# In the steady slots VectorE instead of GpSimd makes the low half of the input, two items ahead

## The chip, the core and the metric

The kernel runs on one core of one Trainium2 chip. The metric is the device time of one execution in microseconds (us). Three runs of the kernel before took 1917.87, 1918.23 and 1918.46 us, median 1918.23 us.

## The reference

The network reads 2048 sequences of 50 steps with 128 features, and one "news" vector for each sequence. Cut to what matters:

```python
hs  = gru(hist, gru_W, gru_U, gru_b)              # 50 steps, 128 units: z, r, candidate
emb = concat([hs, news - hs, news, hs * news])    # attention on each step
a   = relu(emb @ att_W1 + b1); a = relu(a @ att_W2 + b2)
ats = sigmoid(a @ att_W3 + b3)                    # one score for each step and sequence

def au_step(h, xs):                               # second recurrence, over the GRU's states
    u = sigmoid(xu + h @ au_Uu); r = sigmoid(xr + h @ au_Ur)
    c = tanh(xc + r * (h @ au_Uc))
    u_ = at * u
    return (1 - u_) * h + u_ * c
x = batch_norm(concat([h_final, news]))
y = sigmoid(leaky(leaky(x @ d_W1 + d_b1) @ d_W2 + d_b2) @ f_W + f_b)
```

All is float32. The kernel keeps this accuracy by writing a float32 operand as the sum of two float16 halves, `hi` (the value rounded) and `lo` (the value less `hi`), and each weight in the same way. A product is then three float16 products: hi by hi, hi by lo, lo by hi.

## The kernel before

The 2048 sequences are four chunks of 512 (`NC`, `CH`). An item is one chunk at one time step, so there are 200 items, numbered in the order step, chunk: item `i` is chunk `i % 4` at step `i // 4`. The features lie on the 128 partitions and the 512 sequences along the free dimension, so that every elementwise operation works on a 128x512 tile.

The program is written out by hand for each of the five engines, with no scheduler. Each engine runs its own list in order, and semaphores (`wait_ge`, `then_inc`) join the lists. Apart from a short start (items 0 to 13, functions `early`) and an end (`late`, and the dense head), the lists consist of slots, one for each item from 14 (`EARLY`) to 199. Slot `low` does the GRU step of item `low`, the first attention layer of item `low - 2`, and the second recurrence for item `low - 10` (`LAG`) and its neighbours. The loop over slots is unrolled; one slot in four also holds the second attention layer of four items and their scores.

What TensorE does in a slot is fixed in order (lines 1333 to 1400): the attention layer of item `low - 2` (`attention_1`), the reset gate (weights `W_R` on the input x, `U_R` on the state h), the update gate of the second recurrence (`GW_U`, `GU_U`), the candidate's input part, the reset gate and candidate of the second recurrence, the GRU's update gate (`W_Z`, `U_Z`), and two more products. Each product is six matmuls of 64 by 512, two at a time on the two halves of the array. Counted from the code, a slot has 84 of them, and the longer slot 16 more. TensorE waits for `xlo_ready` before the reset gate (line 1343), and for `h_ready` of the item before ahead of `GW_U` (line 1353), since that product overwrites the PSUM bank in which the former update gate stands.

ScalarE does the sigmoids and tanhs and makes most of the `hi` halves. For the input it makes `x_hi` of item `low + 3` in slot `low` (`input_high`, line 682). VectorE does the elementwise steps that read PSUM. GpSimd has no PSUM operand anywhere in this kernel; in a slot it runs, in this order (lines 406 to 425):

- `g_lo`, the low half of the second recurrence's state (line 409),
- `hn`, state times news (line 327), which waits for VectorE's new state h,
- `gus`, update gate times score (line 416),
- `hn_lo` (line 333) and `h_lo` (line 339), low halves, which wait for ScalarE's high halves,
- `d`, old state less candidate (line 423), which VectorE needs for the new state,
- `x_lo`, the low half of the input of item `low + 1` (line 346).

On VectorE the part of a slot around the change is, in order: `a_lo` (line 867), `gt`, reset gate times a product of the second recurrence (line 1027, waits for `gr_ready` from ScalarE), `d` times the update gate z (line 1033, waits for `d_ready` from GpSimd and `z_ready` from ScalarE), a second `gt` step (line 1038) and the new state h (line 1041, which releases `h_ready`). All of these read at least one operand from PSUM.

SyncE's list loads the input: `load_step` waits until `xlo_ready` says that the chunk's buffer in `x32` has been split, and then loads the item four further on. After the third chunk of each step its list also has the two transfers that spread the scores over the partitions, and those wait for scores and for `gus_ready`.

Of the kernel before, what the change touches and what calls it, by code (L numbers as in the profile page):

```python
# [24 lines left out]
ALU = mybir.AluOpType  # L25
# [8 lines left out]
NC = 4  # L34
# [43 lines left out]
def rec_kernel(nc, xs, pack_gru, pack_state, pack_att, pack_rest, out):  # L78
# [14 lines left out]
    EARLY = LAG + NC  # L93
# [6 lines left out]
    def has(item):  # L100
        return 0 <= item < ITEMS

    def pairs_of(low):
        return low % NC == TILED % NC and has(low - TILED)
# [18 lines left out]
    def att_bank(item):  # L123
        return B_GXH if isinstance(item, int) and item < 2 * NC and item % 2 == 0 else B_A1
# [3 lines left out]
    with ExitStack() as ctx:  # L128
        def sb(name, shape, dt=F32):
            return ctx.enter_context(nc.sbuf_tensor(name, shape, dt))  # L130

        def sem(name):
            return ctx.enter_context(nc.semaphore(name))
# [18 lines left out]
        x32 = sb("x32", [P, NC, CH])  # L152
        x_hi = sb("x_hi", [P, NC, CH], F16)
        x_lo = sb("x_lo", [P, NC, CH], F16)
# [61 lines left out]
        xhi_ready, xlo_ready = sem("xhi_ready"), sem("xlo_ready")  # L216
# [99 lines left out]
        def _(pool):  # L316
# [4 lines left out]
            def state_news(item, count):  # L321

                c, k = item % NC, item % 2
                if isinstance(item, int) and item < NC:
                    pool.wait_ge(news_landed[c], 16)
                pool.wait_ge(h_ready, count)
                g.tensor_tensor(hn[:, k, :], h32[:, c, :], news[:, c, :], ALU.mult).then_inc(hn_ready, 1)  # L327

            def state_news_low(item, count):

                k = item % 2
                pool.wait_ge(hnhi_ready, count)
                g.tensor_tensor(hn_lo[:, item % NC, :], hn[:, k, :], hn_hi[:, item % NC, :], ALU.subtract).then_inc(hnlo_ready, 1)  # L333
# [8 lines left out]
            def input_low(item, count):  # L342

                c = item % NC
                pool.wait_ge(xhi_ready, count)
                g.tensor_tensor(x_lo[:, c, :], x32[:, c, :], x_hi[:, c, :], ALU.subtract).then_inc(xlo_ready, 1)  # L346
# [50 lines left out]
            def slot(s0, off):  # L397
                low = off + (s0 if isinstance(s0, int) else LOOP_LO)

                def at(lag):  # L400
                    return s0 + (off - lag + 1)

                def landed(lag):
                    return 4 * (s0 + (off - lag - (low - lag) % NC)) + 16

                if has(low - LAG - 4) and has(low - LAG - 4 + NC):
                    c = (low - LAG - 4) % NC
                    pool.wait_ge(ghi_ready, at(LAG + 4))
                    g.tensor_tensor(g_lo[:, c, :], g32[:, c, :], g_hi[:, c, :], ALU.subtract).then_inc(glo_ready, 1)
                if has(low - 1):  # L410
                    state_news(low - 1, at(1))
                if has(low - LAG - 1):
                    c, k = (low - LAG - 1) % NC, (low - LAG - 1) % 2
                    pool.wait_ge(gu_ready, at(LAG + 1))
                    pool.wait_ge(score_landed, landed(LAG + 1))
                    g.tensor_tensor(gus[:, k, :], gu[:, k, :], score[:, c, :], ALU.mult).then_inc(gus_ready, 1)  # L416
                if has(low - 1):
                    state_news_low(low - 1, at(1))
                    state_low(low - 1, at(1))
                if has(low):  # L420
                    c, k = low % NC, low % 2
                    pool.wait_ge(hc_ready, at(0))
                    g.tensor_tensor(d[:, k, :], h32[:, c, :], hc[:, k, :], ALU.subtract).then_inc(d_ready, EARLY + 1 if low == EARLY else 1)  # L423
                if has(low + 1) and low > EARLY:
                    input_low(low + 1, at(-1))

            for s in range(1, EARLY):
                if s == NC:
# [385 lines left out]
        def _(dve):  # L814
            v = nc.vector
# [47 lines left out]
            def attention_1_low(item, count):  # L863

                k = item % NC
                dve.wait_ge(a1hi_ready, count)
                v.scalar_tensor_tensor(out=a1_lo[:, k, :], in0=ps[:, att_bank(item), :], scalar=0.0,
                                       in1=a1_hi[:, k, :], op0=ALU.max, op1=ALU.subtract).then_inc(a1lo_ready, 1)
# [98 lines left out]
            def slot(s0, off):  # L967
                low = off + (s0 if isinstance(s0, int) else LOOP_LO)

                def at(lag):  # L970
                    return s0 + (off - lag + 1)

                def late(lag):
                    return s0 + (off - lag + 1 - NC)

                if pairs_of(low - 1):
                    low_2(0, paired(s0 + (off - 1)))
                if has(low - 2):
                    attention_1_news(low - 2, at(2))
                if low > EARLY and has(low - LAG - 1):  # L980
                    gated_difference(low - LAG - 1, at(LAG + 1))
                if low > EARLY and pairs_of(low - 1):
                    low_2(1, paired(s0 + (off - 1)))
                if has(low):
                    k = low % 2
                    dve.wait_ge(hh_pe, late(0))
                    dve.wait_ge(r_ready, at(0))
                    v.scalar_tensor_tensor(out=t[:, k, :], in0=ps[:, B_HH, :], scalar=b_hs,
                                           in1=r[:, k, :], op0=ALU.add, op1=ALU.mult).then_inc(t1_ready, 1)
                if low == EARLY:  # L990
                    gated_first(low - LAG - 1, at(LAG + 1))
                elif has(low - LAG - 1):
                    gated_step(low - LAG - 1, at(LAG + 1))
                if has(low):
                    k = low % 2
                    dve.wait_ge(t1_ready, at(0))
                    dve.wait_ge(xh_pe, at(0))
                    v.tensor_tensor(t[:, k, :], t[:, k, :], ps[:, B_XH, :], ALU.add).then_inc(t2_ready, 1)
                if low == EARLY:
                    low_2(1, paired(low - 1))  # L1000
                if low > EARLY and has(low - LAG - 1):
                    gated_state(low - LAG - 1, at(LAG + 1))
                if has(low - 2):
                    attention_1_low(low - 2, at(2))
                known = low if isinstance(s0, int) else None
                if known == BN_LO:
                    bn_eps()
                if known == BN_LO + 1:
                    bn_guess()
                for i in range(NEWTON):  # L1010
                    if known == BN_LO + 3 * i + 2:
                        bn_square(i)
                    if known == BN_LO + 3 * i + 3:
                        bn_error(i)
                    if known == BN_LO + 3 * i + 4:
                        bn_root(i)
                if known == BN_LO + 3 * NEWTON + 2:
                    bn_scale()
                if known == BN_LO + 3 * NEWTON + 3:
                    bn_mean()  # L1020
                if known == BN_LO + 3 * NEWTON + 4:
                    bn_shift()
                if has(low - LAG):
                    k = (low - LAG) % 2
                    dve.wait_ge(ghh_pe, late(LAG))
                    dve.wait_ge(gr_ready, late(LAG))
                    v.tensor_tensor(gt[:, k, :], gr[:, k, :], ps[:, B_GHH, :], ALU.mult).then_inc(gt1_ready, 1)  # L1027
                if known == BN_LO:
                    bn_shift_bits()
                if has(low):  # L1030
                    dve.wait_ge(d_ready, at(0))
                    dve.wait_ge(z_ready, at(0))
                    v.tensor_tensor(ps[:, B_Z, :], d[:, low % 2, :], ps[:, B_Z, :], ALU.mult).then_inc(e_ready, 1)
                if has(low - LAG):
                    k = (low - LAG) % 2
                    dve.wait_ge(gxh_pe, at(LAG))
                    dve.wait_ge(gt1_ready, late(LAG))
                    v.tensor_tensor(gt[:, k, :], gt[:, k, :], ps[:, B_GXH, :], ALU.add).then_inc(gt2_ready, 1)  # L1038
                if has(low):
                    dve.wait_ge(e_ready, at(0))  # L1040
                    v.tensor_tensor(h32[:, low % NC, :], hc[:, low % 2, :], ps[:, B_Z, :], ALU.add).then_inc(h_ready, 1)  # L1041
# [546 lines left out]
```

## Time and profile before

| what | value |
|---|---|
| median of three runs | 1918.23 us (1917.87 to 1918.46) |
| profiled execution, its time | 1917.94 us |
| its span, first to last instruction | 1916.1 us |
| TensorE (PE) busy | 1908.0 us, 100% |
| GpSimd (POOL) busy | 1645.4 us, 86% |
| VectorE (DVE) busy | 1473.6 us, 77% |
| ScalarE (ACT) busy | 1471.6 us, 77% |
| granted TensorE clock | 1.00 through the span |

The time of the profiled execution is 1.84 us more than its span, for what lies ahead of the first and behind the last instruction. An engine's share is its busy time over the span. A row of the timeline gives an instruction's start, its duration, the engine, the line and the tiles; what stands in brackets at its end is the time that the engine sat idle before it, and what it waited for. Durations of successive instructions overlap by a little (the next one begins before the last result of the former is written): VectorE begins one every 0.60 us where it has no wait, though each lasts 0.68 us. The order of the waits is therefore read from starts and ends together.

### The profile page before, as it was taken

The numbers are of one execution on the slowest core, as the hardware profiler recorded it, in microseconds if no ns is written. First come the engines' busy times: TensorE is split into PE (matmuls) and PEld (weight loads), VectorE is DVE, ScalarE is ACT, GpSimd is POOL, SyncE is SP. The second block draws the span as 40 slices with busy tenths as digits, with TensorE's granted clock in tenths as the row PEclk, the third lists the DMA queues.
The fourth block names the chain that finished last, engine by engine and source line by source line (L and its number), as shares of the span: only waits on it lengthen the run. The fifth ranks groups of instructions, "written<-read, shape, count | busy, mean of one in ns | idle before, by whom it ended". The sixth has DMA issues, their size and how long they took to land.

```text
span 1916.1 us, 44510 instructions
## 1 busy us (share of the span) xinstructions
PE 1908.0 (100%) x17607; PEld 999.3 (52%) x17607; DVE 1473.6 (77%) x2324; ACT 1471.6 (77%) x2484; POOL 1645.4 (86%) x1409
## 2 busy tenths in 40 slices
PE   9999999999999999999999999999999999999999
PEld 4555555555555555555555555555555555555554
DVE  7777777777777777777777777777777777787777
ACT  7877777777777777777777777777777777777777
POOL 7888888888888888888888888888888888888886
PEclk9999999999999999999999999999999999999999
DMA  4211121112111211121121112111211121112110
GB/s 131 69 55 53 55 69 54 51 51 73 51 51 51 73 51 50 54 70 50 51 69 55 50 51 73 51 54 53 70 53 51 51 73 51 51 51 73 45 46 23
DMA packets 37911, 110.67 MB, mean 58 GB/s; under 512 B 4348, under 2 KB 4732, under 8 KB 31304
## 3 DMA queue, kind: packets, MB, share of 16 engines
q1 hardware_dynamic: 37560, 107.57, 17.4%
q8 instruction: 140, 2.29, 0.5%
q14 instruction: 67, 0.55, 0.1%
q10 hardware_dynamic: 144, 0.26, 0.1%
HBM read 107.40 MB, written 0.42 MB: 56 GB/s over the span
## 4 chain that ended last, share of the span: by engine, by line
PE 94%; ACT 2%; DVE 1%; POOL 1%; issue 1%; DMA 0%; SPq 0%; DVEq 0%; ACTq 0%; POOLq 0%
PE ps L1149 88%; PE ps L1232 3%; PE ps L1150 1%; PE ps L1223 1%; POOL hn_lo L333 0%; POOL h_lo L339 0%; DMA x<-in_xs 0%; DVE ps L885 0%; DVE ps L879 0%; ACT ps L752 0%; POOL hn L327 0%; ACT ps L575 0%; ACT g_hi L736 0%; ACT a_hi L512 0%; DVE g L890 0%
## 5 line engine op out<-in xcount | busy, mean ns | idle before, releaser
L1149 PE MATMUL ps<-h_hi,w_hi 128*64 128x512 f16 x1384 | 524.6, 379 | 1.9 <-POOL h_lo L339 1.4
L1150 PE MATMUL ps<-h_hi,w_hi 128*64 128x512 f16 x1384 | 524.7, 379 | 0.0
L1150 PE MATMUL ps<-h_lo,w_hi 128*64 128x512 f16 x1384 | 524.5, 379 | 0.0
L1150 PE MATMUL ps<-h_hi,w_lo 128*64 128x512 f16 x1384 | 524.5, 379 | 0.0
L1149 PE MATMUL ps<-h_hi,w_lo 128*64 128x512 f16 x1384 | 524.5, 379 | 0.0
L1149 PE MATMUL ps<-h_lo,w_hi 128*64 128x512 f16 x1384 | 524.5, 379 | 0.0
L333 POOL TENSOR_TENSOR hn_lo<-hn,hn_hi 128x512 f16<-128x512 f32 x200 | 232.4, 1162 | 162.2 <-ACT hn_hi L507 161.8
L327 POOL TENSOR_TENSOR hn<-h,news 128x512 f32<-128x512 f32 x200 | 255.0, 1275 | 74.3 <-DVE h L1041 74.3
L662 ACT ACTIVATE ps<-gt,p_rest 128x512 f32<-128x512 f32 x185 | 127.7, 690 | 199.4 <-DVE gt L1038 199.4
L346 POOL TENSOR_TENSOR x_lo<-x,x_hi 128x512 f16<-128x512 f32 x196 | 226.9, 1158 | 11.8 <-ACT x_hi L527 11.8
L416 POOL TENSOR_TENSOR gus<-gu,score 128x512 f32<-128x512 f32 x186 | 237.0, 1274 | 0.0
L423 POOL TENSOR_TENSOR d<-h,hc 128x512 f32<-128x512 f32 x186 | 236.8, 1273 | 0.0
L1027 DVE TENSOR_TENSOR gt<-gr,ps 128x512 f32<-128x512 f32 x186 | 128.0, 688 | 138.5 <-ACT gr L693 138.5
L339 POOL TENSOR_TENSOR h_lo<-h,h_hi 128x512 f16<-128x512 f32 x200 | 233.2, 1166 | 0.4 <-ACT h_hi L502 0.3
L1149 PE MATMUL ps<-x_hi,w_hi 128*64 128x512 f16 x605 | 229.3, 379 | 0.6 <-DVE a_lo L856 0.6
L1150 PE MATMUL ps<-x_hi,w_hi 128*64 128x512 f16 x605 | 229.3, 379 | 0.0
L1149 PE MATMUL ps<-x_lo,w_hi 128*64 128x512 f16 x605 | 229.3, 379 | 0.0
L1150 PE MATMUL ps<-x_lo,w_hi 128*64 128x512 f16 x605 | 229.3, 379 | 0.0
L1149 PE MATMUL ps<-x_hi,w_lo 128*64 128x512 f16 x605 | 229.3, 379 | 0.0
L1150 PE MATMUL ps<-x_hi,w_lo 128*64 128x512 f16 x605 | 229.3, 379 | 0.0
L1149 PEld LDWEIGHTS ps<-h_hi,w_hi 128*64 128x64 f16 x1384 | 152.2, 110 | 146.1 <-issue 3.0
L1149 PE MATMUL ps<-g_hi,w_hi 128*64 128x512 f16 x596 | 225.9, 379 | 1.1 <-DVE g_lo L1097 1.1
(191 smaller groups left out, 6756.4 us busy)
## 6 DMA issues: line engine op xcount, KB each, us to landing
x<-in_xs SPq DMA_DIRECT2D x199, 256.0 KB, 3.0
score<-score_rows SPq DMA_DIRECT2D x48, 1024.0 KB, 4.7
news<-in_xs SPq DMA_DIRECT2D x4, 256.0 KB, 5.3
x<-score_rows SPq DMA_DIRECT2D x1, 1024.0 KB, 4.6
h<-score_rows SPq DMA_DIRECT2D x1, 1024.0 KB, 5.1
score_rows<-s_rows SPq DMA_DIRECT2D x50, 8.0 KB
p_rest<-in_pack_rest SPq DMA_DIRECT2D x1, 776.0 KB, 7.0
p_att<-in_pack_att SPq DMA_DIRECT2D x1, 291.0 KB, 5.3
```

The costliest lines, as they stand in the source:

```text
L327: g.tensor_tensor(hn[:, k, :], h32[:, c, :], news[:, c, :], ALU.mult).then_inc(hn_ready, 1)
L333: g.tensor_tensor(hn_lo[:, item % NC, :], hn[:, k, :], hn_hi[:, item % NC, :], ALU.subtract).then_inc(hnlo_ready, 1)
L339: g.tensor_tensor(h_lo[:, item % HIST, :], h32[:, c, :], h_hi[:, item % HIST, :], ALU.subtract).then_inc(hlo_ready, 1)
L346: g.tensor_tensor(x_lo[:, c, :], x32[:, c, :], x_hi[:, c, :], ALU.subtract).then_inc(xlo_ready, 1)
L416: g.tensor_tensor(gus[:, k, :], gu[:, k, :], score[:, c, :], ALU.mult).then_inc(gus_ready, 1)
L423: g.tensor_tensor(d[:, k, :], h32[:, c, :], hc[:, k, :], ALU.subtract).then_inc(d_ready, EARLY + 1 if low == EARLY else 1)
L662: a.activation(ps[:, B_GXH, :], gt[:, (low - LAG - 1) % 2, :], ACT.Tanh, bias=b_gated[:, 2:3]).then_inc(gc_ready, 1)
L1027: v.tensor_tensor(gt[:, k, :], gr[:, k, :], ps[:, B_GHH, :], ALU.mult).then_inc(gt1_ready, 1)
L1149: m.matmul(ps[0:H, bank, :], weights[:, 0:H], moving, start=start, stop=stop)
L1150: return m.matmul(ps[H:P, bank, :], weights[:, H:P], moving, start=start, stop=stop)
L1223: done = m.matmul(ps[p * H:(p + 1) * H, bank, :], w3_pair[:, :], part[:, p, :], start=part is a2_hi, stop=part is a2_lo)
L1232: done = m.matmul(ps[k * H:(k + 1) * H, B_PAIR[p], :], w[:, A_2, 0:H], a1[:, 2 * p + k, :], start=w is w_hi and a1 is a1_hi, stop=a1 is a1_lo)
```

## The change

In the slots, `x_lo` moves from GpSimd to VectorE, and one item further ahead: GpSimd made it for item `low + 1` as the last thing of its slot; now VectorE makes it for item `low + 2`, between `a_lo` and `gt`. In slot 14 the new instruction also waits until GpSimd's own last `x_lo` (item 15, in the start) is done. The start (`early`) is unchanged, so items up to 15 are split as before. ScalarE, TensorE and SyncE have the same lists; the lines below the change are numbered four higher.

```diff
@@ GpSimd, slot
                     g.tensor_tensor(d[:, k, :], h32[:, c, :], hc[:, k, :], ALU.subtract).then_inc(d_ready, EARLY + 1 if low == EARLY else 1)
-                if has(low + 1) and low > EARLY:
-                    input_low(low + 1, at(-1))
@@ VectorE, slot
                 if has(low - 2):
                     attention_1_low(low - 2, at(2))
+                if has(low + 2):
+                    c = (low + 2) % NC
+                    dve.wait_ge(xhi_ready, at(-2))
+                    if low == EARLY:
+                        dve.wait_ge(xlo_ready, low + 2)
+                    v.tensor_tensor(x_lo[:, c, :], x32[:, c, :], x_hi[:, c, :], ALU.subtract).then_inc(xlo_ready, 1)
```

VectorE's list in an ordinary slot before, from `a_lo` to the new state:

```order
L867 SCALAR_TENSOR_TENSOR a_lo<-ps,a_hi 128x512 [waits a1hi_ready]
L1027 TENSOR_TENSOR gt<-gr,ps 128x512 [waits gr_ready,ghh_pe]
L1033 TENSOR_TENSOR ps<-d,ps 128x512 [waits z_ready,d_ready]
L1038 TENSOR_TENSOR gt<-gt,ps 128x512 [waits gt1_ready,gxh_pe]
L1041 TENSOR_TENSOR h<-hc,ps 128x512 [waits e_ready]
```

And the same place of VectorE's list now:

```order
L865 SCALAR_TENSOR_TENSOR a_lo<-ps,a_hi 128x512 [waits a1hi_ready]
L1008 TENSOR_TENSOR x_lo<-x,x_hi 128x512 [waits xhi_ready]
L1031 TENSOR_TENSOR gt<-gr,ps 128x512 [waits gr_ready,ghh_pe]
L1037 TENSOR_TENSOR ps<-d,ps 128x512 [waits z_ready,d_ready]
L1042 TENSOR_TENSOR gt<-gt,ps 128x512 [waits gt1_ready,gxh_pe]
L1045 TENSOR_TENSOR h<-hc,ps 128x512 [waits e_ready]
```

One instruction is new, ahead of the four that lead to the state. Both of its inputs lie in SBUF; the other five have one in PSUM.

GpSimd's list before, from the end of one slot into the next:

```order
L339 TENSOR_TENSOR h_lo<-h,h_hi 128x512 [waits hhi_ready]
L423 TENSOR_TENSOR d<-h,hc 128x512 [waits hc_ready]
L346 TENSOR_TENSOR x_lo<-x,x_hi 128x512 [waits xhi_ready]
L409 TENSOR_TENSOR g_lo<-g,g_hi 128x512 [waits ghi_ready]
L327 TENSOR_TENSOR hn<-h,news 128x512 [waits h_ready]
```

And GpSimd's list now:

```order
L339 TENSOR_TENSOR h_lo<-h,h_hi 128x512 [waits hhi_ready]
L423 TENSOR_TENSOR d<-h,hc 128x512 [waits hc_ready]
L409 TENSOR_TENSOR g_lo<-g,g_hi 128x512 [waits ghi_ready]
L327 TENSOR_TENSOR hn<-h,news 128x512 [waits h_ready]
L416 TENSOR_TENSOR gus<-gu,score 128x512 [waits score_landed,gu_ready]
```

`g_lo` follows `d` directly, and a slot of GpSimd has six instructions where it had seven. The whole of VectorE's list has 184 instructions more (2323 before, 2507 now) and GpSimd's 184 fewer.

## Rows read from the trace of the kernel before

**Rows 1.** The page's first part: busy time, share of the span, instructions.

```profile
PE 1908.0 (100%) x17607; PEld 999.3 (52%) x17607; DVE 1473.6 (77%) x2324; ACT 1471.6 (77%) x2484; POOL 1645.4 (86%) x1409
```

**Rows 2.** Busy time by stretch: from:to, length, each engine's busy us, clock, DMA.

```profile
95.00:105.00 10.00, 9.72 (x90) 5.11 (x88) 7.79 (x13) 7.33 (x13) 9.12 (x9) 1.00 0.21 83
...
122.92:160.90 37.98, 37.98 (x354) 19.95 (x352) 29.18 (x47) 29.04 (x49) 33.02 (x29) 1.00 0.17 57
```

**Rows 3.** Timeline, TensorE in a steady slot: start, duration, tiles (one half each).

```profile
1132.42 0.38 PE L1149 MATMUL ps<-h_hi,w_hi 128*64 128x512 f16 x1
...
1132.63 0.38 PE L1149 MATMUL ps<-h_lo,w_hi 128*64 128x512 f16 x1
...
1132.85 0.38 PE L1149 MATMUL ps<-h_hi,w_lo 128*64 128x512 f16 x1
...
1133.07 0.38 PE L1149 MATMUL ps<-h_hi,w_hi 128*64 128x512 f16 x1
```

**Rows 4.** Timeline, VectorE in the same ordinary slot, from a_lo to the state.

```profile
1127.46 0.69 DVE L867 SCALAR_TENSOR_TENSOR a_lo<-ps,a_hi 128x512 f16<-128x512 f32 x1
1128.90 0.69 DVE L1027 TENSOR_TENSOR gt<-gr,ps 128x512 f32<-128x512 f32 x1 [0.75 <-ACT gr L693]
1130.15 0.69 DVE L1033 TENSOR_TENSOR ps<-d,ps 128x512 f32<-128x512 f32 x1 [0.56 <-ACT ps L696]
1130.76 0.68 DVE L1038 TENSOR_TENSOR gt<-gt,ps 128x512 f32<-128x512 f32 x1
1131.36 0.68 DVE L1041 TENSOR_TENSOR h<-hc,ps 128x512 f32<-128x512 f32 x1
```

**Rows 5.** Timeline, GpSimd beside it.

```profile
1127.11 1.16 POOL L339 TENSOR_TENSOR h_lo<-h,h_hi 128x512 f16<-128x512 f32 x1
1128.22 1.27 POOL L423 TENSOR_TENSOR d<-h,hc 128x512 f32<-128x512 f32 x1
1129.45 1.16 POOL L346 TENSOR_TENSOR x_lo<-x,x_hi 128x512 f16<-128x512 f32 x1
1130.57 1.16 POOL L409 TENSOR_TENSOR g_lo<-g,g_hi 128x512 f16<-128x512 f32 x1
1132.12 1.28 POOL L327 TENSOR_TENSOR hn<-h,news 128x512 f32<-128x512 f32 x1 [0.39 <-DVE h L1041]
```

**Rows 6.** Timeline, ScalarE beside it: the gates for which VectorE waits.

```profile
1128.13 0.67 ACT L693 ACTIVATE gr<-ps,p_rest 128x512 f32<-128x512 f32 x1
...
1129.39 0.66 ACT L696 ACTIVATE ps<-ps,b_zr 128x512 f32<-128x512 f32 x1 [0.59 <-PE ps L1150]
```

**Rows 7.** Timeline of the start: VectorE's own x_lo (L1056), with GpSimd beside it.

```profile
17.95 0.68 DVE L1056 TENSOR_TENSOR x_lo<-x,x_hi 128x512 f16<-128x512 f32 x1
...
19.61 1.27 POOL L327 TENSOR_TENSOR hn<-h,news 128x512 f32<-128x512 f32 x1
20.05 1.38 DVE L1056 TENSOR_TENSOR x_lo<-x,x_hi 128x512 f16<-128x512 f32 x1 [1.42 <-ACT x_hi L527]
20.84 1.60 POOL L339 TENSOR_TENSOR h_lo<-h,h_hi 128x512 f16<-128x512 f32 x1
```

**Rows 8.** Timeline of slot 14, the first one, and TensorE behind it.

```profile
93.97 1.16 POOL L339 TENSOR_TENSOR h_lo<-h,h_hi 128x512 f16<-128x512 f32 x1
93.98 0.68 DVE L867 SCALAR_TENSOR_TENSOR a_lo<-ps,a_hi 128x512 f16<-128x512 f32 x1
95.09 1.27 POOL L423 TENSOR_TENSOR d<-h,hc 128x512 f32<-128x512 f32 x1
...
96.40 0.70 DVE L1033 TENSOR_TENSOR ps<-d,ps 128x512 f32<-128x512 f32 x1
...
97.60 0.68 DVE L1041 TENSOR_TENSOR h<-hc,ps 128x512 f32<-128x512 f32 x1
...
98.34 0.40 PE L1149 MATMUL ps<-h_hi,w_hi 128*64 128x512 f16 x1 [0.28 <-DVE h L1041]
```

**Rows 9.** Timeline, GpSimd in the longer slot of the same period.

```profile
1116.92 1.16 POOL L333 TENSOR_TENSOR hn_lo<-hn,hn_hi 128x512 f16<-128x512 f32 x1 [2.16 <-ACT hn_hi L507]
```

## The prediction

> **What bounds the kernel now.** I read the shares first, then the busy time by stretch, then the timeline of one period, engine by engine. The shares put TensorE at 100% and GpSimd, from which work is taken, at 86% [rows 1]. By stretch, a steady period of four slots lasts 37.98 us, and TensorE is busy in all of it, GpSimd in 33.02, VectorE in 29.18 [rows 2]. The timeline confirms that this is a bound and no waiting in disguise: matmuls start every 0.215 us, two at a time, whether the next one reads h_hi, h_lo or begins another product [rows 3]. An engine that waited for an operand would show a longer step somewhere.
>
> The Trainium skill (Perfetto Trace Analysis, Identifying the Most-Contended Engine) speaks against reading it so: matmuls are pipelined, so their busy time misleads, and the busy share of the weight loads is the better measure. That share is 52% here [rows 1]; the even step of 0.215 us is what decides against the rule, since it leaves no gap for another engine to close.
>
> What can be lost or won is therefore a question of slack. In the steady slot the nearest consumer on TensorE is the product that waits for `h_ready`. VectorE ends h at 1131.36 + 0.68 = 1132.04, and TensorE starts that product at 1133.07, from its own order and without a wait [rows 3, 4]. So h may come up to 1.03 us later before TensorE loses anything.
>
> **The change part by part.**
>
> *GpSimd loses x_lo.* 184 instructions of 1.16 us go, a step of 1.12 us each from 1129.45 to 1130.57 [rows 5]. Behind it stand `g_lo` and then `hn`, and `hn` already waits 0.39 us for h [rows 5]. So the freed time turns into a longer wait ahead of `hn`, and no consumer gets anything sooner by it except x_lo itself. It is worth nothing, as TensorE waits for none of GpSimd's results in the period. SyncE's loads wait on `xlo_ready` and go out about a slot earlier; nothing in a full TensorE period can use that either.
>
> *VectorE gains x_lo.* The trace has the same operation on VectorE in the start. Undisturbed it takes 0.68 us. Once it met a GpSimd instruction: it started at 20.05, GpSimd's `hn` ended at 19.61 + 1.27 = 20.88, and x_lo ended at 21.43, 0.55 us behind that. GpSimd's next instruction, queued with no gap, took 1.60 us in place of 1.16, or 0.44 more [rows 5, 7]. So the two engines exclude each other for this form. VectorE waits for the GpSimd instruction that runs, goes next, and the following GpSimd instruction is held for 0.44 us.
>
> The Trainium skill (SBUF — State Buffer, Who interferes with whom) says this as a rule: a VectorE instruction with two SBUF inputs and a GpSimd instruction that reads SBUF exclude each other on a shared port, and whichever issues second is blocked until the first ends. The rows agree for that single meeting. The page does not say who goes next when GpSimd has more queued; both answers are worked out below.
>
> Now the steady slot. `a_lo` starts at 1127.46, and VectorE's step is 0.60 us (1130.76 to 1131.36), so x_lo would ask at 1128.06 [rows 4]. GpSimd then runs `h_lo`, until 1127.11 + 1.16 = 1128.27 [rows 5]. x_lo ends at 1128.27 + 0.55 = 1128.82. The next on VectorE, `gt`, waits for ScalarE's gate until 1128.13 + 0.67 = 1128.80, and started at 1128.90 after 0.75 us of idling [rows 4, 6]. With the overlap of 0.08 between instructions it could start at 1128.74 behind x_lo; so it stays at 1128.90. The 0.75 us wait is the cover, and it is nearly used up.
>
> The `d` on GpSimd is held 0.44 us and ends at 1128.22 + 1.27 + 0.44 = 1129.93 [rows 5]. VectorE needs it at line 1033, but also z, which ScalarE ends at 1129.39 + 0.66 = 1130.05 [rows 6]. z is still later, by 0.12 us. Hence h ends at 1132.04 as before, and the slot costs 0. The longer slot has the same order behind `a_lo`; there GpSimd's `hn_lo` sits 2.16 us until ScalarE's `hn_hi` [rows 9], so that a late GpSimd is put right once in four slots.
>
> *The first slot.* Here there is no cover: the chain runs through GpSimd's `d` to h and TensorE, which stood 0.28 us for h [rows 8]. x_lo asks at 93.98 + 0.60 = 94.58, `h_lo` ends at 95.13, and `d` is held 0.44 us, until 95.09 + 1.27 + 0.44 = 96.80. Lines 1033 and 1041 and TensorE's product at 98.34 each move by 0.44. `gt` between them needs x_lo's end at 95.68, which is sooner than that. This is the only term: +0.44 us.
>
> *Sum.* Against the profiled execution's 1917.94 us: 184 slots at 0, and 0.44 once, gives 1918.38, say 1918.4 us. The median of the runs shown, 1918.23, lies 0.29 above the profiled time, so in terms of the runs the forecast is 1918.4 to 1918.7; the runs themselves spread over 0.59 us.
>
> *Bounds.* The unknown cost is one x_lo on VectorE beside a GpSimd that has more queued. The nearest rows are 0.68 and 1.38 us [rows 7]; I take 0.76, from 1128.06 to 1128.82, because it meets only the last 0.21 us of `h_lo`. It asks just 0.16 us ahead of `d` (1128.06 against 1128.22), and if it loses that race it waits for all of `d`. The end on that side: x_lo ends at 1128.22 + 1.27 + 0.55 = 1130.04, `gt` starts at 1129.96, lines 1033, 1038 and 1041 follow in steps of 0.60, and h starts at 1131.76, 0.40 late. That leaves 0.63 of the 1.03 us: still 0 for TensorE in a steady slot. In the first slots, where there is less slack, up to three slots may pay it: 3 x 0.40 = 1.20 more, or 1919.6. On the other side the most that TensorE could get back between 95 and 105 us is its idle 0.28 us [rows 2], or 1917.7.
>
> **The rivals.**
>
> *x_lo loses the race to `d` in most slots.* For it speaks the margin of 0.16 us. Then VectorE's x_lo shows about 1.9 us long and h is 0.40 late, and the time is 1918.4 to 1919.6, since the 1.03 us holds. The kernel would stand closer to its edge with nothing to show for it in time.
>
> *GpSimd keeps the port while it has work queued: slower.* Then x_lo waits through `d` and the `g_lo` that now follows it directly, until GpSimd stops for h. `g_lo` would run from 1129.45 to 1130.61, x_lo end at 1131.16, and h at 1131.16 - 0.08 + 3 x 0.60 + 0.68 = 1133.56, behind TensorE's 1133.07. From there each slot is a closed ring: h, six GpSimd instructions, x_lo, four on VectorE, h. GpSimd's mean is 33.02 over 28 in the period, 1.18 us, and six are 7.08; then 0.55, then 2.40 from x_lo's end to h's, and 0.08 from h to `hn`: 10.11 us. TensorE's mean slot is 37.98 / 4 = 9.50. The loss is 0.61 x 184 = 112 us, or 2030 us. It decides as soon as VectorE is not served between two queued GpSimd instructions. Against it: at 20.84 `h_lo` was queued behind `hn` with no gap, and VectorE went between [rows 7]. But that is one meeting, and here there are 184.
>
> *TensorE has room, and the freed GpSimd gives time: faster.* At most it could give GpSimd's whole step, 1.12 x 184 = 206 us, or 1712 us; a tenth of it would be seen. The even step of the matmuls [rows 3] and `hn`'s wait for h [rows 5] speak against any of it.
>
> **How the numbers follow.** The forecast case has 0.65. Losing the race to `d` has 0.23. The held port has 0.08, and with it lies all of slower. Faster has 0.02. The last 0.02 is for a gain of the 0.28 us, which no run could tell. A measurement of this kernel tells about 0.2%, or 3.8 us, from no change, so the first two cases and the last are "same": 0.90. The range takes the bounds 1917.7 and 1919.6 with the spread of the runs, 0.59, on either side: 1917.1 to 1920.2. The held port, 112 us away, is left out.
>
> **What the new profile would show.** If right: TensorE's steady period is still 37.98 us and its step 0.215; VectorE has an x_lo of about 0.76 us between `a_lo` and `gt`, and the 0.75 us wait for `gr` is all but gone; `d` on GpSimd lasts about 1.7 us; `hn` waits for h 1.0 to 1.1 us in place of 0.39; and TensorE's idle at 98 us grows from 0.28 to about 0.72. An x_lo of about 1.9 us with `d` at 1.27 and `g_lo` longer would be the lost race. x_lo ending only behind `g_lo`, and TensorE waiting for h in every slot, would make the prediction wrong.

## The result, and the profile after

The changed kernel takes 1925.21 us (median of five executions, 1925.15 to 1926.93). Beside it on the same chip the kernel before takes 1918.23 us (1917.50 to 1920.19). The ratio is 1.0038, with a 95% interval of 1.0026 to 1.0049. So the change makes the kernel slower by some 7 us. The forecast of 1918.4 us was wrong, and the upper end of its range, 1920.2, was missed by 5.0 us.

The profiled execution of the changed kernel took 1925.15 us, its span is 1923.4 us. Against the profiled execution of before that is 7.21 us more. The page's first part answers to [rows 1]:

```profile
PE 1909.3 (99%) x17607; PEld 999.1 (52%) x17607; DVE 1619.6 (84%) x2508; ACT 1468.2 (76%) x2484; POOL 1523.6 (79%) x1225
```

TensorE has the same work and is no longer at 100%. The list of waits (engine, line, waited for: us in total, times, longest) says for whom it now stands (it lists idle time of over 0.15 us):

```profile
POOL hn L327 <- DVE h L1045: 215.7, 186, 2.5
...
PE ps L1153 <- DVE h L1045: 5.5, 7, 0.8
```

Before, TensorE waited once for the new state h, 0.28 us [rows 8]. Now it waits seven times. The busy time by stretch (from:to, length, busy us of PE, PEld, DVE, ACT, POOL, clock, DMA share, GB/s) tells where:

```profile
1149.20:1187.18 37.98, 37.98 (x354) 19.95 (x352) 31.82 (x51) 29.05 (x49) 30.35 (x25) 1.00 0.17 56
...
1756.99:1794.98 37.99, 36.34 (x334) 18.52 (x332) 35.99 (x52) 26.81 (x48) 28.08 (x23) 1.00 0.17 57
```

The first row answers to the period of [rows 2]: TensorE is full, as before. Fifteen successive stretches of this length, from 1149.20 to 1719.00, read so. The three after them, to 1832.96, read like the second row: TensorE lacks 1.6 us in each, and 18 to 20 of its matmuls no longer fit in. The loss lies in three of the last periods, and in one slot at the beginning.

This is an ordinary steady slot of the changed kernel, VectorE, GpSimd and the TensorE product that needs h, in the timeline; it answers to [rows 3 to 5]:

```profile
140.46 0.69 DVE L865 SCALAR_TENSOR_TENSOR a_lo<-ps,a_hi 128x512 f16<-128x512 f32 x1
141.06 0.74 DVE L1008 TENSOR_TENSOR x_lo<-x,x_hi 128x512 f16<-128x512 f32 x1
141.21 1.73 POOL L423 TENSOR_TENSOR d<-h,hc 128x512 f32<-128x512 f32 x1
141.90 0.69 DVE L1031 TENSOR_TENSOR gt<-gr,ps 128x512 f32<-128x512 f32 x1
142.90 1.16 POOL L409 TENSOR_TENSOR g_lo<-g,g_hi 128x512 f16<-128x512 f32 x1
143.15 0.69 DVE L1037 TENSOR_TENSOR ps<-d,ps 128x512 f32<-128x512 f32 x1 [0.56 <-ACT ps L694]
...
144.35 0.68 DVE L1045 TENSOR_TENSOR h<-hc,ps 128x512 f32<-128x512 f32 x1
...
145.11 1.28 POOL L327 TENSOR_TENSOR hn<-h,news 128x512 f32<-128x512 f32 x1 [1.06 <-DVE h L1045]
...
146.06 0.38 PE L1153 MATMUL ps<-h_hi,w_hi 128*64 128x512 f16 x1
```

It is the slot that was forecast, to the hundredths: x_lo 0.74 us, d held to 1.73, z still the later one ahead of line 1037, `hn` waiting 1.06, and h ending at 145.03, 1.03 us before TensorE's product. Slot 14 is the forecast one too (answers to [rows 8]):

```profile
94.77 1.11 DVE L1008 TENSOR_TENSOR x_lo<-x,x_hi 128x512 f16<-128x512 f32 x1
95.28 1.73 POOL L423 TENSOR_TENSOR d<-h,hc 128x512 f32<-128x512 f32 x1
...
97.04 0.70 DVE L1037 TENSOR_TENSOR ps<-d,ps 128x512 f32<-128x512 f32 x1 [0.57 <-POOL d L423]
...
98.98 0.40 PE L1153 MATMUL ps<-h_hi,w_hi 128*64 128x512 f16 x1 [0.73 <-DVE h L1045]
```

TensorE's idle time there grew from 0.28 to 0.73, or 0.45 us. That leaves 7.21 - 0.45 = 6.8 us for the late periods. There a slot of the changed kernel looks so:

```profile
1731.79 0.68 DVE L1045 TENSOR_TENSOR h<-hc,ps 128x512 f32<-128x512 f32 x1
1732.54 1.28 POOL L327 TENSOR_TENSOR hn<-h,news 128x512 f32<-128x512 f32 x1 [1.37 <-DVE h L1045]
...
1736.96 0.69 DVE L865 SCALAR_TENSOR_TENSOR a_lo<-ps,a_hi 128x512 f16<-128x512 f32 x1
1737.28 1.27 POOL L423 TENSOR_TENSOR d<-h,hc 128x512 f32<-128x512 f32 x1
1737.56 1.54 DVE L1008 TENSOR_TENSOR x_lo<-x,x_hi 128x512 f16<-128x512 f32 x1
1738.51 1.60 POOL L409 TENSOR_TENSOR g_lo<-g,g_hi 128x512 f16<-128x512 f32 x1
1739.02 1.11 DVE L911 SCALAR_TENSOR_TENSOR bn_t<-bn_t 128x2 f32<-128x2 f32 x1
1740.06 0.67 DVE L1031 TENSOR_TENSOR gt<-gr,ps 128x512 f32<-128x512 f32 x1
...
1741.39 0.38 PE L1153 MATMUL ps<-h_hi,w_lo 128*64 128x512 f16 x1
1741.85 0.68 DVE L1045 TENSOR_TENSOR h<-hc,ps 128x512 f32<-128x512 f32 x1
...
1742.58 0.40 PE L1153 MATMUL ps<-h_hi,w_hi 128*64 128x512 f16 x1 [0.80 <-DVE h L1045]
```

Between x_lo and `gt` stands an instruction that the prediction did not count: a step of the batch norm's inverse root, two values on each partition. The functions `bn_eps` to `bn_shift` (lines 895 to 928) are such steps, and one of them stands in each slot from 184 to 197 (`BN_LO`; slot 184 has a second one behind `gt`), in the code behind the new x_lo and ahead of `gt`. The same step in the timeline of the kernel before:

```profile
1735.85 0.21 DVE L913 SCALAR_TENSOR_TENSOR bn_t<-bn_t 128x2 f32<-128x2 f32 x1
1736.01 1.27 POOL L423 TENSOR_TENSOR d<-h,hc 128x512 f32<-128x512 f32 x1
1736.69 0.69 DVE L1027 TENSOR_TENSOR gt<-gr,ps 128x512 f32<-128x512 f32 x1 [0.62 <-ACT gr L693]
```

It took 0.21 us in the wait for the gate, just ahead of d. Now it takes 1.11. Both of its inputs lie in SBUF, as those of x_lo do, and it has to wait for GpSimd as x_lo does. An instruction is said to ask when it starts in the timeline. x_lo asks behind d and waits for it, and by the time that the small step asks, `g_lo` has asked already: the step waits until `g_lo` ends. From a_lo to h it takes 1741.85 - 1736.96 = 4.89 us where the ordinary slot takes 144.35 - 140.46 = 3.89, so h is 1.00 us later on that path. One such slot alone would still fit into the 1.03 us of slack; the loss comes from handing the delay on. GpSimd waits for h with `hn`, then runs without a gap to the end of `g_lo`, `g_lo` holds the small step, and the small step holds the next h. That closes a ring, a chain in which each h waits for the one before: h starts at 1721.75, 1731.79, 1741.85 and 1751.90, one every 10.05 us, where TensorE's mean slot is 9.50. Four turns are 40.2 us in place of 37.99, and TensorE's waits show the same distance: one period after the row at 1742.58 comes

```profile
1782.78 0.40 PE L1153 MATMUL ps<-h_hi,w_hi 128*64 128x512 f16 x1 [0.80 <-DVE h L1045]
```

or 40.20 us later, and the next comes at 1823.00, 40.22 after that. Three such periods (12 slots) cost 3 x 2.22 = 6.7 us; with slot 14's 0.45 that is 7.1 of the 7.21.

The waits in the list are shorter than the loss, because they count only from the end of the matmul before. From start to start, TensorE's step is 1742.58 - 1741.39 = 1.19 us in place of 0.215, or 0.97 more. That happens in two slots of a late period. In a third the step is 0.43 us (1772.30 to 1772.73), too little idle time for the list. Together 0.97 + 0.97 + 0.21 = 2.15 of the 2.22 us. In the longer slot of each late period the chain is another: x_lo asks ahead of d there, the small step waits for d (1.22 us), and GpSimd waits 1.08 us for ScalarE's `hn_hi`. Why h comes after some 10.05 us in that slot too, no run here shows.

### The profile page after: what moved, and what is told of

Its sections match the earlier page's. It is cut to its first block, busy times and chain, and to the rows that moved or that the text cites. A ratio compares the mean times of both kernels' runs of the same rounds, so it can differ in the third digit from the quotient of the medians.

```text
span 1923.4 us, 44511 instructions
## 1 busy us (share of the span) xinstructions
PE 1909.3 (99%) x17607; PEld 999.1 (52%) x17607; DVE 1619.6 (84%) x2508; ACT 1468.2 (76%) x2484; POOL 1523.6 (79%) x1225
## 4 chain that ended last, share of the span: by engine, by line
PE 89%; POOL 4%; ACT 3%; DVE 2%; issue 2%; DMA 0%; SPq 0%; DVEq 0%; POOLq 0%; ACTq 0%
PE ps L1153 83%; PE ps L1236 3%; PE ps L1154 1%; PE ps L1227 1%; POOL hn L327 1%; POOL hn_lo L333 1%; POOL h_lo L339 1%; POOL d L423 1%; POOL g_lo L409 0%; POOL gus L416 0%; ACT ps L573 0%; DVE gt L1042 0%; DMA x<-in_xs 0%; ACT a_hi L510 0%; POOL x_lo L346 0%
## 5 line engine op out<-in xcount | busy, mean ns | idle before, releaser
L423 POOL TENSOR_TENSOR d<-h,hc 128x512 f32<-128x512 f32 x186 | 312.2, 1678 | 0.0
L1153 PE MATMUL ps<-g_hi,w_hi 128*64 128x512 f16 x596 | 225.9, 379 | 1.1 <-DVE g_lo L1101 1.1
L1154 PE MATMUL ps<-g_hi,w_hi 128*64 128x512 f16 x596 | 225.9, 379 | 0.0
L1153 PE MATMUL ps<-g_lo,w_hi 128*64 128x512 f16 x596 | 225.9, 379 | 0.0
```

Source lines behind the costliest of these rows:

```text
L1153: m.matmul(ps[0:H, bank, :], weights[:, 0:H], moving, start=start, stop=stop)
L1154: return m.matmul(ps[H:P, bank, :], weights[:, H:P], moving, start=start, stop=stop)
```

## Experiments

The theory after the result: the loss is the batch norm's steps behind x_lo, because VectorE then meets GpSimd twice ahead of `gt`, and a slot has room for one such meeting in which VectorE has to wait. I held at first that the number of meetings counts, whatever their order; the first rival is that the order of asking decides. Others are that x_lo alone is too much, that anything more on VectorE behind x_lo would do the same, and that the engines take turns.

**The batch norm's steps elsewhere (e1).** They go from behind x_lo to VectorE's wait for the reset gate r, half a slot earlier.

```diff
                 if low > EARLY and has(low - LAG - 1):
                     gated_difference(low - LAG - 1, at(LAG + 1))
+                known = low if isinstance(s0, int) else None
+                if known == BN_LO:
+                    bn_eps()
...
@@ behind x_lo
-                known = low if isinstance(s0, int) else None
-                if known == BN_LO:
-                    bn_eps()
...
```

> The changed kernel, with the small batch-norm instructions of slots 184 to 197 (128x2, one a slot) moved to a place ahead of VectorE's wait for r, away from x_lo. Theory (port): TensorE's loss between 1719 and 1833 us comes from two VectorE instructions in a row that each have to let one GpSimd instruction by; with x_lo alone each slot pays one, and the loss of 6.7 us goes. Expected 1918.3 to 1919.2 us: the before plus the 0.45 of slot 14; no wait of TensorE for h after 100 us. Rival (load): VectorE is simply too full with x_lo and the small ones in these slots; moving them within the slot changes nothing, 1925 us.

Measured: 1918.74 us (1918.08 to 1920.65), ratio to before 1.0004, interval 0.9995 to 1.0013. The step and what follows it in VectorE's list, and the stretch that had lacked 1.6 us:

```profile
1734.47 0.22 DVE L911 SCALAR_TENSOR_TENSOR bn_t<-bn_t 128x2 f32<-128x2 f32 x1
...
1735.36 0.75 DVE L1004 SCALAR_TENSOR_TENSOR t<-ps,p_gru,r 128x512 f32<-128x512 f32 x1 [0.67 <-ACT r L645]
```

```profile
1719.00:1756.99 37.99, 37.99 (x354) 19.95 (x352) 32.29 (x55) 29.05 (x50) 30.37 (x25) 1.00 0.17 57
```

The step is back at 0.22 us with 0.67 us of idling behind it, TensorE is full, and its only wait for h is the one of slot 14. The 6.7 us are gone with nothing else moved: it was these steps behind x_lo, not x_lo alone.

**The steps ahead of x_lo (e2).** The same block directly between a_lo and x_lo; number and kind of the meetings stay.

```diff
                     attention_1_low(low - 2, at(2))
+                known = low if isinstance(s0, int) else None
+                if known == BN_LO:
+                    bn_eps()
...
                 if has(low + 2):
                     c = (low + 2) % NC
...
-                known = low if isinstance(s0, int) else None
...
```

> The changed kernel, with the small batch-norm instructions between a_lo and x_lo, so that x_lo follows them. Theory (port): the number of meetings counts and not their order; the small one waits for d, then x_lo for g_lo, which costs 0.44 us a slot more than the other order, because the longer of the two now comes last. Expected as slow as the change or slower, 1925 to 1930 us. Rival (order): the small instruction is the one that comes too late behind x_lo; ahead of it, it takes 0.22 us in the end of h_lo and the loss goes, 1918.3 to 1920 us.

Measured: 1918.66 us (1918.20 to 1920.33), ratio 1.0004, interval 0.9995 to 1.0013. My theory, that the number of meetings counts, fell here; the rival, that the order decides, held. The timeline:

```profile
1738.19 0.21 DVE L911 SCALAR_TENSOR_TENSOR bn_t<-bn_t 128x2 f32<-128x2 f32 x1
1738.33 0.68 DVE L1026 TENSOR_TENSOR x_lo<-x,x_hi 128x512 f16<-128x512 f32 x1
1738.34 1.79 POOL L423 TENSOR_TENSOR d<-h,hc 128x512 f32<-128x512 f32 x1
1739.03 0.69 DVE L1031 TENSOR_TENSOR gt<-gr,ps 128x512 f32<-128x512 f32 x1
```

Both VectorE instructions ask before d, x_lo by 0.01 us, and both go through at their undisturbed 0.21 and 0.68; d waits for them. From here on the theory is that the one who asks first is served first, and that a step is dear where GpSimd has asked in between.

**The small step in every slot, behind x_lo (e4).** If the steps of 14 slots cost 6.7 us, a like one in all slots must cost it in all. The added product is not used.

```diff
                     v.tensor_tensor(x_lo[:, c, :], x32[:, c, :], x_hi[:, c, :], ALU.subtract).then_inc(xlo_ready, 1)
+                v.tensor_tensor(tiny[:, low % NC, :], b_zr[:, :], b_zr[:, :], ALU.mult)
```

> The changed kernel, with one more instruction of 128x2 with two SBUF inputs behind x_lo in every slot (its result is not used). Theory (port): every period of four slots does what the three of the batch norm did, 40.21 us in place of 37.99: 2.22 x 46 = 102 us, plus up to 1.2 us in each of the 13 slots that now have three such instructions; 2015 to 2040 us. Rival (load): it costs VectorE its own 0.22 us, which the slack of the slots covers outside the batch-norm slots: 1925 to 1930 us.

Measured, one execution: 2023.04 us, 98 us more than the changed kernel; the executions of one kernel lie within 3 us of each other here. In a steady slot, and in the list of waits:

```profile
1120.46 1.54 DVE L1009 TENSOR_TENSOR x_lo<-x,x_hi 128x512 f16<-128x512 f32 x1
1121.40 1.61 POOL L410 TENSOR_TENSOR g_lo<-g,g_hi 128x512 f16<-128x512 f32 x1
1121.92 1.11 DVE L1028 TENSOR_TENSOR tiny<-b_zr 128x2 f32<-128x2 f32 x1
1122.95 0.67 DVE L1033 TENSOR_TENSOR gt<-gr,ps 128x512 f32<-128x512 f32 x1
```

```profile
PE ps L1155 <- DVE h L1047: 76.6, 96, 1.2
```

It is the row of the batch norm's slots again, and TensorE waits in two slots of each period. By the ring, 46 periods x 2.22 us are 102 us on 1918.4, or 2020.5 us; in the slots from 184 on a third instruction of this kind comes on top.

**The same place, one input in PSUM (e5).** An instruction as small, but with one of its two inputs in PSUM, tells whether it is one more instruction that costs, or the meeting with GpSimd.

```diff
+                dve.wait_ge(ghh_pe, late(LAG))
+                v.tensor_tensor(tiny[:, low % NC, :], b_zr[:, :], ps[:, B_GHH, 0:2], ALU.mult)
```

> The changed kernel, with one more 128x2 instruction behind x_lo in every slot, as in the run that took 2023 us, but with one input in PSUM and one in SBUF. Theory (port): it needs nothing that GpSimd holds, takes about 0.2 us, and lies in the cover of the slots; in the 13 slots of the batch norm it lengthens the ring by its step of 0.1 to 0.2 us. 1925 to 1928 us. Rival (load): any further VectorE instruction at this place does it: 2010 to 2040 us.

Measured: 1926.39 us (1926.19 to 1928.00), ratio to before 1.0045, interval 1.0030 to 1.0060; about 1.2 us on the changed kernel, not 98.

```profile
1129.92 0.14 DVE L1029 TENSOR_TENSOR tiny<-b_zr,ps 128x2 f32<-128x2 f32 x1
```

0.14 us in place of 1.11: it is the second SBUF input that is dear, not one more instruction.

**The small step in the kernel before (e6).** The product of e4 in every slot of the kernel before, behind a_lo, where no x_lo stands.

```diff
                     attention_1_low(low - 2, at(2))
+                v.tensor_tensor(tiny[:, low % NC, :], b_zr[:, :], b_zr[:, :], ALU.mult)
```

> The kernel before (x_lo on GpSimd), with the 128x2 instruction with two SBUF inputs behind a_lo in every slot. Theory (port): it asks in the last 0.2 us of h_lo and ahead of d, as the batch-norm instructions of slots 187 to 197 do in the trace of before (0.21 us each), inside the 0.75 us wait for gr: 1918 to 1919 us, the same as before. Only together with x_lo does it cost 2.2 us a period. Rival: a two-SBUF instruction costs a GpSimd instruction's length wherever it stands: 0.4 us late in h, still no loss, but it then shows 1.0 us or more long.

Measured: 1918.03 us (1917.74 to 1918.59), ratio 0.9999, interval 0.9990 to 1.0009. In a steady slot it lasts 0.21 us, asks 0.16 us ahead of d, and lies in the wait for the gate, of which 0.62 us is left. In ten slots it asks behind d and lasts 1.0 to 1.25 us, and TensorE's only wait for h is still the 0.28 us of slot 14. Without x_lo beside it the small step does no harm, in time or late.

**x_lo elsewhere (e7).** The batch norm's steps stay; x_lo goes to VectorE's wait for r.

```diff
+                if has(low + 2):
+                    c = (low + 2) % NC
...
                 if low > EARLY and pairs_of(low - 1):
                     low_2(1, paired(s0 + (off - 1)))
...
-                if has(low + 2):
-                    c = (low + 2) % NC
...
```

> The changed kernel, with x_lo itself moved to a place ahead of VectorE's wait for r (0.80 us of idling in an ordinary slot), and the batch-norm instructions where they were. Theory (port): x_lo then meets hn or gus, whose delay of 0.44 us is covered; the small instructions have the place behind a_lo to themselves, as before the change. No TensorE wait for h in the steady slots and none added in slot 14: 1918.0 to 1918.8 us, the same as before. Rival (load): VectorE does the same work as in the change, so 1925 us.

Measured: 1918.85 us (1918.17 to 1920.44), ratio 1.0005, interval 0.9996 to 1.0013; the median lies 0.05 above the span expected. x_lo lasts 0.76 us there and holds GpSimd's `gus` to 1.72. The batch norm's steps do not go back to 0.21 us, as the expectation implied: behind a_lo they ask behind d in each of the 14 slots and last 1.01 to 1.14 us. TensorE still has no wait in these slots, and its wait in slot 14 is the 0.28 us of before. One instruction in a slot that asks too late costs nothing here; it takes two.

**Order against turns (e9), and a late x_lo (e8).** Both stand on e1. In e9 the two-input product of e4 stands ahead of x_lo; in e8 the one-PSUM product of e5 stands there, to make x_lo ask behind d.

```diff
+                v.tensor_tensor(tiny[:, low % NC, :], b_zr[:, :], b_zr[:, :], ALU.mult)
                 if has(low + 2):
                     c = (low + 2) % NC
```

> The changed kernel with the batch-norm instructions in the r wait, and in every slot the 128x2 instruction with two SBUF inputs, ahead of x_lo and not behind it. Theory (first asked, first served): the small one and x_lo both ask ahead of d, and d waits for both; 1918.3 to 1920 us against 2023 with the other order. Rival (turns: VectorE has to let one GpSimd instruction by after each of its own that needs the port): as slow as the other order, 2010 to 2040 us.

Measured: 1919.23 us (1918.57 to 1921.48), ratio 1.0008, interval 0.9999 to 1.0018, where the other order of the same two instructions, in e4, took 2023. (e4 also leaves the batch norm's steps behind x_lo, but those alone cost the changed kernel no more than 6.7 us.) A steady slot:

```profile
1128.78 0.21 DVE L1022 TENSOR_TENSOR tiny<-b_zr 128x2 f32<-128x2 f32 x1
1128.91 0.68 DVE L1028 TENSOR_TENSOR x_lo<-x,x_hi 128x512 f16<-128x512 f32 x1
1128.93 1.79 POOL L424 TENSOR_TENSOR d<-h,hc 128x512 f32<-128x512 f32 x1
```

d asks 0.02 us behind x_lo and waits for it: first asked, first served. If turns were taken, d would have gone between the two. The same run has the other case too: in 18 slots d asked 0.19 to 0.29 us ahead of the small step, and there the step lasts 1.00 to 1.09 us.

For e8 the expectation was:

> The changed kernel with the batch-norm instructions in the r wait (the run that took 1918.74 us), and a 128x2 instruction with one PSUM input ahead of x_lo in every slot, which makes x_lo ask 0.1 to 0.2 us later, behind GpSimd's d. Theory (first asked, first served): x_lo loses to d in most slots and shows 1.3 us or more; h comes 0.4 to 0.6 us late, inside the 1.03 us that TensorE has; 1918.3 to 1920 us. Rival: the 1.03 us is eaten and TensorE waits for h: 1925 us or more.

Measured: 1919.35 us (1918.30 to 1920.66), ratio 1.0007, interval 0.9997 to 1.0016. It missed its aim: the added instruction moved x_lo by 0.08 us only (1130.26 to 1130.34), d asked at 1130.38, and x_lo lasted 0.69 us. Its time says nothing of a lost race.

**The lost race in every slot (e10).** So the added product of e8, with one PSUM input, is made 256 columns long (the lines stand against e8).

```diff
-                v.tensor_tensor(tiny[:, low % NC, :], b_zr[:, :], ps[:, B_GHH, 0:2], ALU.mult)
+                v.tensor_tensor(tiny[:, :], news[:, 0, 0:256], ps[:, B_GHH, 0:256], ALU.mult)
```

> The changed kernel with the batch-norm instructions ahead of VectorE's wait for r, and in every slot an added 128x256 product with one PSUM input between a_lo and x_lo, so that x_lo asks some 0.2 us behind GpSimd's d instead of 0.02 to 0.16 us ahead of it. Theory (first asked, first served; the lost race is paid from slack): x_lo lasts 1.3 us or more, d stays near 1.27, g_lo is held at about 1.6, h comes 0.4 to 0.7 us later than in the changed kernel, and TensorE still does not wait in the steady slots, because the ring of one slot (h, five GpSimd instructions of 1.18 us to d, 0.55, 2.40 from x_lo's end to h's, 0.08: 8.93 us) stays under TensorE's 9.50; time 1918.3 to 1920.5. Rival (the margin is already too small for a lost race): h is over 1.03 us late, TensorE waits for h in most periods and each long one costs some 2 us as in slots 184 to 197 of the changed kernel; time 1960 to 2025.

Measured: 1918.84 us (1918.49 to 1920.26), ratio 1.0004, interval 0.9995 to 1.0014. A steady slot, and the TensorE product behind it:

```profile
1128.93 1.28 POOL L424 TENSOR_TENSOR d<-h,hc 128x512 f32<-128x512 f32 x1
1129.18 0.41 DVE L1023 TENSOR_TENSOR tiny<-news,ps 128x256 f32<-128x256 f32 x1
1129.51 1.25 DVE L1029 TENSOR_TENSOR x_lo<-x,x_hi 128x512 f16<-128x512 f32 x1
1130.17 1.61 POOL L410 TENSOR_TENSOR g_lo<-g,g_hi 128x512 f16<-128x512 f32 x1
...
1132.48 0.68 DVE L1048 TENSOR_TENSOR h<-hc,ps 128x512 f32<-128x512 f32 x1
...
1133.78 0.38 PE L1156 MATMUL ps<-h_hi,w_hi 128*64 128x512 f16 x1
```

x_lo asks 0.58 us behind d's start and ends with d plus 0.55 (1130.21, 1130.76); `g_lo` is the one held. h ends at 1133.16, and 0.62 us of slack is left, 0.41 less than in the ordinary slot of the changed kernel. x_lo lost in 183 of its 184 slots, and TensorE's one wait for h is the 0.73 us of slot 14: one lost race in a slot costs TensorE nothing.

## Why the prediction was wrong

*TensorE bounds the kernel, and a steady slot has 1.03 us of slack behind h.* Right outside the last three periods: 37.98 us as before, and 1.03 us in the changed slot.

*GpSimd's freed time is worth nothing.* Right: `hn` waits 1.06 us in place of 0.39, within the forecast 1.0 to 1.1.

*x_lo 0.76 us, d held to 1.7, the gate's wait used up, z still later.* Right in the ordinary slots: in 165 of the 184 x_lo asks ahead of d and lasts 0.73 to 0.75 us, and d 1.71 to 1.74; line 1037 waits for z.

*Slot 14 costs 0.44 us.* Right: 0.45.

*A lost race costs h 0.40 us and TensorE nothing in a steady slot; at most three first slots pay.* Right and on the safe side. Slots 15 to 17 and five later ones (29, 103 to 105, 157) did lose it, with x_lo at 1.54 to 1.63 us, and TensorE did not wait in them. e10 shows 0.41 us of slack spent in a steady slot, and no loss. The sign "about 1.9 us" for such an x_lo was mis-added (1130.04 - 1128.06 is 1.98), and the real one is shorter, since x_lo asks 0.20 to 0.28 us behind d's start and not at the time forecast.

*"184 slots at 0".* This step failed. I read one ordinary slot and one longer slot and took them for all 184. The 0.75 us wait that I called "nearly used up" is not empty in slots 184 to 197: there the batch norm's steps stood in it, each of which can be held by GpSimd too. With x_lo ahead of them they ask too late, and last 1.11 to 1.23 us where most had taken 0.21. With the late h, x_lo loses its race to d as well in the ordinary slots that follow (185, 187 to 189, and so on to 197), and the ring turns at 10.05 us. Three periods pay 2.22 us each. That is the whole miss, by e1 and e2, which take it away by moving nothing but these steps.

*The rival of the held port.* Its sum was good and its mechanism was not. It gave a ring of 10.11 us with all six GpSimd instructions in it; 10.05 was measured. That they agree so well is in part luck: the sum has x_lo's 0.55 us behind `g_lo`, where the trace has the small step and a `g_lo` held for 0.44. GpSimd does not keep the port while it has work queued: VectorE is served between d and `g_lo`, as [rows 7] had it. The ring closes because VectorE has to be served twice in a slot, and `g_lo` asks in between. I had made it a matter of all slots or none, at 112 us, and so left out of the range the case of a few slots; e4 is the case of all of them, at 2023 us against the rival's 2030.

It could have been read in the trace of before. A list of VectorE's instructions by line shows the batch norm's 128x2 steps, at 0.21 us in the most part, but at 1.13 and 1.06 us for the two of lines 901 and 905, which had met GpSimd already; each of these has a single input in SBUF. The Trainium skill (SBUF — State Buffer, Who interferes with whom) has the rule that bears on the steps with two inputs: it goes by the number of inputs in SBUF and by who issues first, not by an instruction's size. The rows of 0.21 and 1.11 us agree.

What stays open: no variant is faster than the kernel before. The six with x_lo on VectorE that avoid the loss lie 0.5 to 1.2 us in the median above the kernel before as measured beside them, within what their intervals can tell from none, and no run here has a steady period below 37.98 us.

## What to carry to other kernels

A wait that is to hide a new instruction has to be read in every slot in which the instruction will stand, the few unusual ones too; list all that the engine runs between the two neighbours, not only what the sample slot shows. Where two engines exclude each other, find every user of the shared resource on both lists and write down who asks when: here the small step lasted 0.21 us where it asked in time, and 1.0 to 1.25 us where it asked too late, if only by 0.02 us (e6), and waited for the rest of the other engine's instruction. A small instruction of that kind is better placed ahead of a large one (e2), or in another wait (e1). A delay that fits into the slack once can still cost time if each slot hands it to the next.

## What the runs showed of the hardware that I had not expected

In these runs whoever asked first was served first. A lead of 0.01 us (e2) or 0.02 us (e9) was enough for VectorE; on the other side 0.02 us was enough for d: in one slot of e6 it started at 120.75 and the small step, which then lasted 1.25 us, at 120.77. Two VectorE instructions that both ask in time go through one after the other, and GpSimd's waits for both: d took 1.79 us in those rows in place of 1.27.

A lost race cost a small instruction as much as a large one. 128x2 values took 1.11 us behind a `g_lo`, 0.90 more than undisturbed; x_lo with 128x512 took 1.54 us behind a d, 0.86 more than its undisturbed 0.68. With one of its inputs in PSUM the small one took 0.14 us.

Even a step with one SBUF input can be held. The first one of the batch norm, in the timeline of the changed kernel:

```profile
1707.73 1.71 POOL L423 TENSOR_TENSOR d<-h,hc 128x512 f32<-128x512 f32 x1
1708.24 1.23 DVE L895 TENSOR_SCALAR bn_t<-p_rest 128x2 f32<-128x2 f32 x1
```

It ends at 1709.47, 0.03 us behind d; in the kernel before it took 0.22 us. The Trainium skill (SBUF — State Buffer, Who interferes with whom) counts `tensor_scalar` among the operations that can enter a faster mode with two ports, and can then contend with GpSimd. The row agrees that it can be held; in which mode it ran, no run shows.
